# Macaron block on one core: the product rm·u left in its PSUM bank, norm statistics as single pieces, new order tables

## The reference, cut to what matters

```python
x = x + 0.5 * ffn(layernorm(x))
x = x + attn(layernorm(x))
x = x + 0.5 * ffn(layernorm(x))

# ffn: HIDDEN = 768
h = silu(x @ wg.T) * (x @ wu.T);  return h @ wd.T

# attn
z = x @ W_z.T;  params = x @ W_params.T;  C = params[..., r + n:]
dt = softplus(params[..., :r] @ W_dt.T + b_dt)
u = silu(causal_conv4(x, conv_w));  A = -exp(A_log)
a = exp(dt * A);  b = (a - 1) / A
h[t] = a[t-1] * h[t-1] + b[t-1] * u[t-1]          # 16 states per channel
y = sum_n(C[n] * h[n]) + u * D
return (y * silu(z)) @ W_out.T
```

## Time and profile before

| | |
|---|---|
| median of 3 runs | 2453.26 us (2450.96 to 2454.65) |
| the profiled execution: its own time / its span | 2457.36 us / 2455.6 us |
| busy in the span: DVE / PE / POOL / ACT | 93% / 92% / 84% / 83% |
| mean granted TensorE clock | 0.956 of full speed |
| first scan / last scan starts at | 102.1 us / 2403.6 us |
| DMA | 291 MB, mean 119 GB/s |

### The profile page before, as it was taken

One profiled execution on the slowest core, in us unless ns is written; L12 is line 12 of the kernel. 1 busy time (PEld: TensorE's weight loads), 2 busy tenths in 40 slices (PEclk: granted clock), 3 DMA queues, 4 the chain that ended last, 5 costly groups with the idle time before them and its releaser, 6 DMA issues. The chain is left out here.

```text
span 2455.6 us, 28769 instructions
## 1 busy us (share of the span) xinstructions
PE 2258.3 (92%) x9220; PEld 1359.8 (55%) x9220; DVE 2282.8 (93%) x2454; ACT 2030.5 (83%) x2926; POOL 2073.5 (84%) x1286
## 2 busy tenths in 40 slices
PE   6977999999999999999999999999999999999578
PEld 3443656556565555656556565655656555565346
DVE  2599999999999999999999999999999999999993
ACT  4888888988888797988989888898888889898662
POOL 1588988989898898889989898898988889899873
PEclk9997999999999899999999899999999999999789
DMA  2122433434343343434434243343434334333221
GB/s 68 49 78 59 135 130 129 138 126 139 106 154 130 120 139 112 145 116 142 140 122 146 100 149 130 129 138 129 138 106 151 131 129 138 122 129 114 84 65 39
DMA packets 112027, 291.21 MB, mean 119 GB/s; under 512 B 11201, under 2 KB 45314, under 8 KB 111874
## 3 DMA queue, kind: packets, MB, share of 16 engines
q1 hardware_dynamic: 111874, 289.35, 35.7%
HBM read 271.49 MB, written 17.83 MB: 118 GB/s over the span
## 5 line engine op out<-in xcount | busy, mean ns | idle before, releaser
L996 POOL TENSOR_TENSOR acc<-acc,ring 128x1024 f32<-128x1024 f32 x512 | 1209.5, 2362 | 146.7 <-DVE ring L1178 134.2
L1142 DVE TENSOR_TENSOR_SCAN g_bank<-du_bank,ring 128x1024 f32<-128x1024 f32 (+1 forms) x512 | 1100.6, 2155 | 7.3 <-ACT du_bank L903 0.5
L674 PE MATMUL work<-wd_t,hid 128*128 128x256 f32 x3072 | 697.7, 386 | 37.1 <-DVE hid L1099 35.5
L1178 DVE SCALAR_TENSOR_TENSOR ring<-g_bank,inv_a,ring 128x1024 f32<-128x1024 f32 (+1 forms) x576 | 664.6, 1159 | 11.4
L674 PEld LDWEIGHTS work<-wd_t,hid 128*128 128x128 f32 x3072 | 590.0, 193 | 153.4 <-DVE hid L1099 43.6
L921 ACT ACTIVATE ring<-dt,a_coef 128x1024 f32<-128x1024 f32 (+1 forms) x576 | 577.4, 1047 | 7.0 <-DVE g_bank L1142 4.1
L742 ACT ACT_TABLE_LOAD x289 | 370.8, 1283 | 5.1
L662 PE MATMUL work<-xt_hi,wu_t 128*128 128x512 f16 x768 | 304.9, 397 | 26.9 <-ACT xt_lo L793 14.4
L662 PE MATMUL work<-xt_hi,wg_t 128*128 128x512 f16 x768 | 299.7, 390 | 29.4 <-ACT sil L806 14.5
L662 PE MATMUL work<-xt_lo,wu_t 128*128 128x512 f16 x768 | 304.3, 396 | 0.0
L662 PE MATMUL work<-xt_lo,wg_t 128*128 128x512 f16 x768 | 298.8, 389 | 0.0
(11 more groups left out here) (96 smaller groups left out, 2797.9 us busy)
## 6 DMA issues: line engine op xcount, KB each, us to landing
ring<-c_rows SPq DMA_DIRECT2D x448, 512.0 KB, 3.6
ring<-c_rows SPq DMA_DIRECT2D x64, 256.0 KB, 3.1
x_in<-L_attn_x SPq DMA_DIRECT2D x30, 512.0 KB, 5.4
out<-x_fin SPq DMA_DIRECT2D x30, 512.0 KB, 5.2
c_rows<-params SPq DMA_DIRECT2D x32, 32.0 KB, 3.0
x_fin<-L_attn_x SPq DMA_DIRECT2D x2, 512.0 KB, 4.4
out<-x_in SPq DMA_DIRECT2D x2, 512.0 KB, 2.9
ring<-L_ffn_w_gate SPq DMA_DIRECT2D x1, 768.0 KB, 5.8
```

The costliest lines, as they stand in the source:

```text
L674: last = pe.matmul(dst[:, j * E:(j + 1) * E], hid[:, K.unit[f, bt, c, m] % HIDS, t:t + P], wd_t[:, m, :], start=(m == 0), stop=(m == HM - 1))
L996: nc.gpsimd.tensor_tensor(v, v, shaped(bt, cg[:, K.number[ev[1:]] % TERMS, :]), ALU.add).then_inc(S["summed"], 1)
L1142: scan = nc.vector.tensor_tensor_scan(g, du_h, d_h, first[0], ALU.add, ALU.mult)
L1178: nc.vector.scalar_tensor_tensor(v, g, inv_a[:, h, s:s + 1], c_row, ALU.mult, ALU.mult).then_inc(S["weighted"], 1)
```

## The change

- `ai` is split. Its first instruction now writes the product back into the PSUM bank that it read. Its second, now an event of its own, `aj`, reads the product from the bank and u from SBUF, writes acc, and frees the bank. The waits that hung on acc_begun hang on the freed bank; two waits on ACT name all jobs that they used to imply.
- The four bn_stats of a norm become four events `sj` with places of their own, each with its own wait for the half of the rows that it reads (`rp` or `ra` of its pair j // 2) and its own semaphore step. `ln` keeps the four bn_aggr.
- All three tables (ROW, HEAD, TAIL) hold new numbers. With them ACT's order has 315 table loads where it had 289 (20 in place of 18 in most batches).

```diff
 ROW = {
-    "ln1": [-43.875, -42.278],
+    "sj1": [-48.467, -48.349, -46.751, -46.532, -45.253, -44.701, -44.618, -44.043],
+    "ln1": [-45.903, -43.644],
...
-    "ai": [-4.711, -5.166, -4.862, -3.977],
+    "ai": [-4.535, -5.253, -5.217, -3.21],
+    "aj": [-3.998, -4.782, -4.712, -2.696],
...
         return ({"ga": "si", "dn": "rs", "op": "rc", "z": "zs", "pm": "pe", "cv": "us", "dt": "da",
-                 "rm": "ai"}[job[0]],) + job[1:]
+                 "rm": "aj"}[job[0]],) + job[1:]
...
-                    wait(act, "acc_begun", ("ai", bt - 2, EH - 1, NC - 1))
+                    for k in range(EH * NC):
+                        wait(act, "free", ("rm", bt - 2, k // NC, k % NC))
...
-                    wait(act, "ready", ("rm", bt - 1, EH - 1, c))
+                    for h in range(EH):
+                        wait(act, "ready", ("dt", bt - 1, h, c))
+                        wait(act, "ready", ("rm", bt - 1, h, c))
...
-                            wait(pool, "acc_begun", ("ai", bt, k, p) if paired(bt) else ("ai", bt, p, k))
+                            wait(pool, "free", ("rm", bt, k, p) if paired(bt) else ("rm", bt, p, k))
...
+                    if kind == "sj":
+                        _, f, bt, c, j = ev
...
+                            wait(dve, "mid_added", ("rp", bt, c, j // 2))
...
+                        nc.vector.bn_stats(stats[:, slot, j, :], src[:, c * TJ + j, :]).then_inc(S["stats"], 1)
+                    elif kind == "ln":
+                        slot = K.at["meanvar", ev][1] % 2
+                        wait(dve, "stats", ("sj",) + ev[1:] + (TJ - 1,))
...
-                        nc.vector.tensor_tensor(t, bank(job)[:], u[bt % 2][:, h, 1 + c * CH:1 + (c + 1) * CH],
-                                                ALU.mult).then_inc(freed(job), 1)
-                        wait(dve, "free", job)
-                        nc.vector.scalar_tensor_tensor(t, u[bt % 2][:, h, 2 + c * CH:2 + (c + 1) * CH], d_skip[:, h:h + 1], t,
-                                                       ALU.mult, ALU.subtract).then_inc(S["acc_begun"], 1)
+
+                        nc.vector.tensor_tensor(bank(job)[:], bank(job)[:], u[bt % 2][:, h, 1 + c * CH:1 + (c + 1) * CH],
+                                                ALU.mult).then_inc(S["times_u"], 1)
+                    elif kind == "aj":
+                        _, bt, h, c = ev
+                        job = ("rm",) + ev[1:]
+                        wait(dve, "times_u", ("ai",) + ev[1:])
+                        nc.vector.scalar_tensor_tensor(acc[bt % 2][:, h, c * CH:(c + 1) * CH],
+                                                       u[bt % 2][:, h, 2 + c * CH:2 + (c + 1) * CH], d_skip[:, h:h + 1],
+                                                       bank(job)[:], ALU.mult, ALU.subtract).then_inc(freed(job), 1)
```

More of the change, by code:

```diff
@@ L77 @@
 ROW = {
[59 rows of a table removed]
[L137 to L149, removed]
@@ L150 @@
-    "op": [35.343, 35.563, 38.067, 38.279],
-    "rc": [34.543, 34.806, 36.425, 37.971],
-    "ra": [34.196, 35.385, 37.281, 40.898],
[65 rows of a table added]
+    "gate": [16.606, 31.868],
+    "scan": [-0.221, 2.45, 2.836, 3.033, 4.469, 5.728, 6.381, 6.993, 7.919, 8.53, 10.246, 11.093, 11.942, 12.707,
+        15.362, 15.797, 16.645, 17.819, 18.525, 19.878, 20.717, 21.259, 21.534, 22.62, 22.988, 23.783, 24.781,
+        26.454, 27.903, 29.006, 30.587, 31.124],
+    "cm": [-0.055, 2.46, 2.91, 3.267, 5.222, 6.239, 6.612, 7.286, 8.146, 9.481, 10.947, 11.798, 12.142, 14.228,
+        15.62, 16.476, 17.209, 18.197, 18.78, 20.055, 21.046, 21.457, 21.796, 22.886, 23.653, 24.047, 25.747, 27.402,
+        28.724, 30.446, 30.657, 31.278],
@@ new lines @@
+    "bc": [-1.46, 0.233, 0.889, 2.005, 2.933, 3.103, 5.929, 5.98, 9.245, 10.873, 11.17, 11.889, 12.185, 12.277,
+        12.532, 12.745, 13.449, 14.267, 15.726, 16.443, 17.201, 17.729, 18.256, 19.565, 20.534, 24.139, 24.285,
+        24.506, 25.329, 26.087, 26.971, 29.845],
+    "ex": [-0.92, -0.697, -0.282, -0.046, 2.894, 3.236, 4.948, 5.569, 5.675, 5.678, 6.956, 7.312, 9.835, 13.022,
+        13.055, 13.185, 13.524, 13.788, 13.845, 14.108, 14.285, 20.462, 20.581, 20.594, 20.961, 22.85, 23.165,
+        23.181, 23.327, 25.008, 28.594, 29.35],
@@ L153 @@
+    "op": [34.131, 37.803, 38.472, 39.054],
+    "rc": [33.255, 36.73, 36.802, 39.789],
+    "ra": [34.271, 35.729, 35.776, 39.572],
 }
 HEAD = {
[L156 to L195, removed]
+    "sj1": [-122.701, -108.214, -105.892, -95.055, -56.545, -52.866, -50.101, -40.707],
+    "ln1": [-80.273, -40.531],
+    "lr1": [-88.835, -51.814],
+    "ls1": [-72.986, -40.117],
+    "lx1": [-79.454, -56.766],
@@ new lines @@
+    "T1": [-65.673, -37.469],
+    "Te1": [-78.571, -38.077],
+    "Ts1": [-55.241, -36.39],
+    "Tl1": [-78.01, -36.637],
+    "sj2": [-30.408, -23.999, -22.628, -22.151, -4.978, -4.588, -3.088, -2.428],
+    "ln2": [-22.092, -1.143],
+    "lr2": [-13.99, -4.702],
+    "ls2": [-21.49, 0.928],
+    "lx2": [-21.851, 1.35],
+    "T2": [-16.389, 4.903],
+    "Te2": [-21.374, 2.79],
+    "ga1": [-50.173, -46.906, -46.554, -42.355, -36.772, -30.465, -30.461, -23.295, -17.668, -17.564, -17.56,
+        -12.241],
@@ new lines @@
+    "si1": [-50.352, -40.411, -40.544, -38.903, -33.045, -36.557, -26.97, -31.858, -22.867, -21.865, -21.044,
+        -10.692],
+    "up1": [-49.407, -45.71, -39.763, -33.286, -26.059, -23.023, -22.708, -20.356, -17.684, -16.427, -11.01, -2.894],
+    "sc1": [-55.538, -36.924, -34.514, -30.62, -22.053, -9.26],
+    "hp1": [-50.192, -33.574, -33.219, -23.051, -12.342, -11.011],
+    "sh1": [-37.451, -34.619, -32.341, -25.106, -18.417, -9.313],
+    "dn1": [-22.592, -21.375, -1.473, -0.253],
+    "rs1": [-30.832, -23.372, -4.453, -2.278],
@@ new lines @@
+    "rp": [-31.642, -27.926, -5.794, -5.76],
+    "pm": [-15.548, 6.258],
+    "pe": [-21.267, 3.962],
+    "cw": [-9.202, 3.887],
+    "cv": [-13.367, 6.383, -9.32, 8.914],
+    "us": [-14.569, 4.156, -8.662, 6.277],
+    "z": [0.972, 11.176, 10.368, 12.283],
+    "zs": [0.643, 18.26, 10.918, 15.154],
+    "dt": [-7.166, 8.488, -1.556, 11.49],
+    "da": [-6.887, 5.551, -5.062, 11.22],
+    "dl": [-5.206, 6.44, -4.49, 12.009],
+    "dp": [-9.258, 7.386, -6.644, 11.898],
+    "rm": [0.53, 11.555, -3.169, 10.118],
@@ L196 @@
+    "ai": [-2.198, 12.202, -9.143, 10.441],
+    "aj": [1.15, 12.848, -5.121, 10.533],
+    "u0": [-8.461],
+    "dt0": [-1.512],
 }
 TAIL = {
[20 rows of a table removed]
[21 rows of a table added]
 }
@@ L240, in row_events @@
         for c in range(NC):
+            for j in range(TJ):
+                yield f"sj{f}", ("sj", f, b, c, j)
             for kind in ("ln", "lr", "ls", "lx", "T", "Te") + (("Ts", "Tl") if f != 2 else ()):
@@ L257, in row_events @@
         for c in range(NC):
-            for kind in ("cv", "us", "z", "zs", "dt", "da", "dl", "dp", "rm", "ai"):
+            for kind in ("cv", "us", "z", "zs", "dt", "da", "dl", "dp", "rm", "ai", "aj"):
                 yield kind, (kind, b, h, c)
@@ L315, in __init__ @@
                 last["dn"] = ev
+            elif kind == "ln":
+                made = [place["sj", ev[1], ev[2], ev[3], j] for j in range(TJ)] + [place[ev]]
+                assert made == sorted(made)
             elif kind == "cv":
@@ L367, in releaser @@
         return ({"ga": "si", "dn": "rs", "op": "rc", "z": "zs", "pm": "pe", "cv": "us", "dt": "da",
-                 "rm": "ai"}[job[0]],) + job[1:]
+                 "rm": "aj"}[job[0]],) + job[1:]
     def increments(self, ev):
         kind = ev[0]
+        if kind == "sj":
+            return [("stats", 1)]
         if kind == "ln":
-            return [("stats", 1), ("meanvar", 1)]
+            return [("meanvar", 1)]
         if kind == "Te":
@@ L384, in increments @@
             return [(f"c_out{ev[2]}", 16)]
-        one = {"db": "du_in", "gate": "gated", "u0": "u_first", "dt0": "dt_first", "ai": "acc_begun",
+        one = {"db": "du_in", "gate": "gated", "u0": "u_first", "dt0": "dt_first", "ai": "times_u",
                "d": "du", "da": "sp_exp", "dl": "sp_ln", "dp": "sp_sum", "si": "silu",
@@ L1064, in program @@
                     kind = ev[0]
-                    if kind == "ln":
-                        _, f, bt, c = ev
-                        slot = K.at["meanvar", ev][1] % 2
+                    if kind == "sj":
+                        _, f, bt, c, j = ev
+                        unit = ("ln", f, bt, c)
+                        slot = K.at["meanvar", unit][1] % 2
                         src = {1: x_of(bt), 2: x_mid[bt % 2], 3: fin(bt)}[f]
@@ L1071, in program @@
                         elif f == 2:
-                            wait(dve, "mid_added", ("rp", bt, c, 1))
+                            wait(dve, "mid_added", ("rp", bt, c, j // 2))
                         else:
-                            wait(dve, "fin_added", ("ra", bt, 2 * c + 1))
+                            wait(dve, "fin_added", ("ra", bt, 2 * c + j // 2))
```

(12 more changed lines are left out.)

## The result

The changed kernel takes 2374.93 us (median of 4 runs, 2370.51 to 2376.00) where the one before takes 2453.30 us (4 runs, 2450.96 to 2454.65): a ratio of 0.9678, with a 95% interval of 0.9662 to 0.9693. The forecast was 2372, the range 2335 to 2415.

The account below looks back on a forecast made before the run. DVE was taken to bound the kernel. Thirteen batches 5.6 us shorter gave 73 us, 83 with the other windows: 2374 from the profiled execution, 2370 from the median, so 2372, range 2335 to 2415.

Parts of the forecast that it names:

- What bounds the kernel before: Middle batches of 145.4 us: DVE has no slack, with 143.5 us of work and gaps and 1.9 of waiting.
- Part one: Second instruction of ai on DVE: product read from PSUM takes 680 ns instead of 1665, saving 3.9 us a batch.
- Part two: DVE order: 25 fewer adjacent pairs that need each other, 0.118 us saved each, 2.95 us a batch.
- Rival (b): DVE gaps: parting pairs saves nothing because DVE drains anyway; period 141.4 us, total 2393; chance 0.08.
- DVE needs 136.6: DVE's need per middle batch after the change: 145.4 less 1.9 of waiting, 3.9 and 2.95 gives 136.6 us.
- PE needs 139.1: PE's need per middle batch, 139.1 us if its clock is granted as before, making it the new limit.
- rival (a): Middle batches: DVE stays the limit, PE's clock falls less, PE needs 135–136; period 137 us, total 2336; chance 0.15.
- changes hands: Middle batches: the limit passes from DVE to PE at 139.1 us a batch, with DVE close behind.
- Period 139.8: Middle batches: new period of 139.8 us, 5.6 less than before, 73 us over 13 batches.
- Batches 0 and 14, 4 us each: Batches 0 and 14, also bound by DVE, each gain 4 us, with fewer pieces to place.
- Tail, 1 gained: Tail: all but the last two of the last norm's four bn_stats can go before the second POOL addition, gaining 1 us.
- Rival (d), banks held longer: rm banks held longer until L1148 stall PE; at a period of 147 us, 21 us slower, total 2476; chance 0.05.

Follow-up runs that it names:

- e2: The kernel before with its old tables, only the product left in its PSUM bank, which the second instruction frees: 2428.56 us, ratio 0.9890.
- e1: The changed kernel with the same tables and bank release, but the product rm times u written to acc in SBUF again: 2401.19 us, ratio 0.978.
- e4: The changed kernel with the norm's four-element shift product moved from DVE to POOL as two small products: 2356.65 us, ratio 0.9598 to the kernel before.
- e5: The changed kernel with eight extra small DVE instructions a batch, each in front of a cm: 2395.91 us, ratio 0.9765 to the kernel before.
- e6: The changed kernel with one extra fp16 matmul per gate product of the first feed-forward, 12 a batch on PE: 2399.32 us, ratio 0.9779 to the kernel before.
- e3: The changed kernel with the four bn_stats of a norm in a block again, at the place of its aggregation: 2447.40 us, ratio 0.9967 to the kernel before.
- e7: The changed kernel with the shift product on POOL and the four bn_stats in a block again: 2376.30 us, ratio 0.9685 to the kernel before.

## Why the prediction came out right

**The time** was 2374.9 us for a forecast of 2372, and the mechanism was the forecast's own. That it came out within 3 us is in part luck: DVE's need was put 1.5 us a batch too low, since one term was missing, and PE's 2.1 too high, and the forecast period rested on both.

- *What bounds the kernel before: DVE, 143.5 us a batch.* Held. With 4.0 us taken off it and nothing else (e2) the batch shortens by 2.0, and DVE waits 1.9 more.
- *Part one, 3.9 us a batch at 0.68 us a piece.* The piece takes 0.73 us, not 0.68: the rows that I priced it from, L1099 and L1118, don't read a number per partition (d_skip), and which of the differences costs the 0.05 is open. The account has 4.05 a batch, since the old mean in the middle batches was above the 1.665 of the whole span (6.97 / 4 = 1.74). e1 shows that the cause is the product in SBUF: same order, same release, only the product moved, which the first instruction writes and the second reads. The second's minimum there is 0.719 us, against 0.718 with the product in PSUM; in the old order it is 0.750 at the least in the kernel before and 0.748 at the median in e2. So with POOL out of the way the place costs nothing, and the 62 cycles between the two columns of the table in the Trainium skill ("VectorE: DVE Perf Modes", the section on the TRN2 errata), which spoke against the edit, showed neither way. The gain is the standing behind POOL, about 1.0 us a piece (1.74 − 0.75) and not 0.8: I had measured it from the 0.86 us of the earlier trace rows, which holds some itself. The PSUM write of the first instruction costs 0.007 us (685 against 678 ns), so nothing, as I took it.
- *Part two, 25 pairs × 0.118 = 2.95 us.* The account has 0.91 + 2.18 = 3.09. Rival (b) falls with it: separated instructions do overlap. The section that I set against the trace there, "The DRAIN you can't avoid" in the Trainium skill ("VectorE: DVE Perf Modes"), says as well that a next instruction that is not held starts earlier, so it doesn't contradict these rows as I had it.
- *The term that failed:* "DVE needs 136.6". It needs 139.55 − 1.44 = 138.1. I priced the moved bn_stats and didn't look at the moved shift product, though it has two inputs in SBUF as L1121 had: 3.44 us a batch in place of 1.05. It was there to be seen: its line before has a minimum of 0.15 us and a maximum of 1.22. All other durations fell by 0.6 us, which I hadn't priced either.
- *PE needs 139.1.* Its busy time is 1781.1 / 13 = 137.0, since the granted clock rose to 0.99. That was the mechanism of rival (a), which thus came half true. With the shift product off DVE the period does go below 139, to 138.6 (e4). That the limit "changes hands" was wrong: e5 and e6 show that it is shared. Of my signs for it, PE's share did pass 97% (1781.1 of 1814.2 us, 98%), but DVE's waits, which should have grown from 1.9 to 3 us a batch, fell to 1.4.
- *Period 139.8:* 139.55. *Batches 0 and 14, 4 us each:* 5.4 and 4.8. *Head, 1:* 3.9 (the first scan at 98.2). *Batch 15, nothing:* 0.8 lost, at a clock of 0.77 in place of 0.82. *Tail, 1 gained:* 2.5 lost. The last window holds 47.5 us of PE work in place of 45.8, and the norm's statistics did start in halves, two behind each addition; why the tail is longer is open. Together 87 us between the profiled spans for a forecast of 83; the medians differ by 78, since the profiled execution was 4 us above its median before and 4 below it after.
- *Rival (d), banks held longer:* small. Who waited for L1148, over the whole span (us, times):

```profile
  PEld work L679: 7.8, 12
  PE work L679: 2.6, 2
```

The weight loads wait some, the matmuls hardly. e2's loss at that place goes the other way, DVE waiting for PE.

The two parts add up over the old and new tables: 25 us for the bank alone (e2), 26 us for it under the new tables (e1 against the changed kernel), 53 us for the new tables and pieces without it (e1 against before).

## What to carry to other kernels

Look at an instruction's spread, not only at its mean: one whose maximum is several times its minimum, and that ends together with an instruction of another engine, may be waiting inside itself, as both were here, and no list of waits shows it. Where there is a choice, give DVE instructions at most one SBUF input while POOL is busy, small ones too; holding the bank through a second instruction was cheaper here. When an order is moved, cost every instruction of that kind in its new place. When two engines are close in load, expect neither all nor nothing of a change to one of them: here three quarters or more of what was added arrived (e5, e6), but of what was taken off DVE only a half (e2: 2.0 of 4.0 us) or a quarter (e4: 0.9 of 3.4).

## What the runs showed that I had not expected

A product of 4 elements a partition takes 0.14 us at the least and 2.3 when POOL began a long sum 0.07 us before it. It made up 3.4 us of a batch of 139.6, and moving it off DVE gave 18 us (e4). With it on DVE a change of order costs 72 us (e3 against the changed kernel), without it 20 (e7 against e4).
